# The last block of a chunked state scan reordered on TensorE and VectorE, with one block's statistics moved into the expert passes

## The reference

```
xn = LN(x)
u  = silu(causal_conv(xn @ Wx.T));  z = xn @ Wz.T              # 512 inner channels, 8 heads of 64
b, c = u @ Wb.T, u @ Wc.T;  dt = softplus(u @ Wdt.T + b_dt)
state_t = exp(dt_t * a) * state_(t-1) + dt_t * b_t (x) u_t     # a 64x64 state for each head
y_t = c_t . state_t + d * u_t
yn = (y - mean) / sqrt(var + eps)                              # over all tokens of a sequence, by head
s  = ((yn * gn_w + gn_b) * silu(z)) @ Wout.T
g  = silu(sum over 8 experts of gate * expert(their 1024 tokens of largest gate))
out = x + s * g
```

## Time and profile before

| | before |
|---|---|
| median of 3 runs | 1240.03 us (1238.38 to 1241.29) |
| the profiled execution | 1240.59 us |
| its span on the core | 1238.4 us |
| PE busy | 1211.5 us, 98% |
| DVE / POOL / ACT busy | 948.0 us, 77% / 792.0 us, 64% / 611.0 us, 49% |
| granted TensorE clock, mean | 0.994 |

### The profile page before, as it was taken

The page is one execution under the profiler, slowest core; times in us unless marked ns, Lnnn a source line. Parts: engine busy times, 40 slices in busy tenths (PEclk is TensorE's granted clock), DMA queues, the critical chain, the costliest instruction groups (busy, mean ns, idle before and its releaser), DMA issues.

```text
span 1238.4 us, 30811 instructions
## 1 busy us (share of the span) xinstructions
PE 1211.5 (98%) x12207; PEld 1015.2 (82%) x12207; DVE 948.0 (77%) x2030; ACT 611.0 (49%) x1277; POOL 792.0 (64%) x788
## 2 busy tenths in 40 slices
PE   8999999999999999999999997899999999999998
PEld 4666677888878888888888876789999889899998
DVE  7999876889876776777777775897778766776776
ACT  6999974434434353443443435334344332554453
POOL 4889845455555577767767755376666654576764
PEclk9999999999999999999999998999999999999999
DMA  9799758553544444454444365464444545799995
GB/s 296 261 339 354 291 201 183 179 168 130 162 156 158 152 153 148 147 180 154 163 162 155 130 196 157 144 148 89 107 95 90 104 86 119 236 321 329 339 321 173
DMA packets 124462, 231.33 MB, mean 187 GB/s; under 512 B 21280, under 2 KB 88096, under 8 KB 116128
## 3 DMA queue, kind: packets, MB, share of 16 engines
q1 hardware_dynamic: 111168, 212.08, 51.0%
q0 software_dynamic: 12288, 17.05, 8.0%
q10 hardware_dynamic: 864, 0.24, 0.1%
HBM read 147.81 MB, written 81.53 MB: 185 GB/s over the span
## 4 chain that ended last, share of the span: by engine, by line
PE 81%; DVE 9%; ACT 3%; issue 2%; DMA 2%; POOL 1%; SPq 1%; POOLq 0%; ACTq 0%; DVEq 0%
PE ps L1390 26%; PE ps L1736 9%; PE ps L1993 9%; PE ps L2227 7%; PE ps L2206 7%; PE ps L1471 4%; PE ps L1438 3%; PE ps L1498 3%; PE ps L1460 3%; PE ps L1482 2%; PE ps L1509 2%; PE ps L695 2%; DVE acc L324 1%; ACT tap L503 1%; DVE acc L335 1%
## 5 line engine op out<-in xcount | busy, mean ns | idle before, releaser
L1357 ACT ACTIVATE decay<-tap,ncum 128x128 f32<-128x128 f32 x344 | 105.5, 389 | 175.6 <-POOL tap L1268 175.6
L1921 POOL DMA_INDIRECT ffn_dram<-ob,idx x64 | 110.3, 1724 | 81.6 <-DVE ob L1840 67.3
L1151 DVE TENSOR_TENSOR x_dt<-ps,dt 128x512 f32<-128x512 f32 x64 | 44.3, 692 | 142.1 <-PE ps L1498 142.1
L1955 ACT ACTIVATE mid<-ps,b_up 128x512 f32<-128x512 f32 x96 | 66.0, 689 | 162.3 <-PE ps L1736 137.4
L1275 POOL TENSOR_TENSOR x_lo<-x,x_hi 128x512 fp32r<-128x512 f32 x56 | 75.4, 1346 | 98.7 <-ACT x_hi L1341 98.5
L1390 PE MATMUL ps<-x_hi,w_hi_c 128*128 128x512 f32 x240 | 99.4, 414 | 1.3 <-DVE state L1103 1.3
L1390 PE MATMUL ps<-x_hi,w_hi_b 128*128 128x512 f32 x240 | 99.9, 416 | 0.7 <-ACT bT L1346 0.7
L1297 POOL TENSOR_SCALAR yb<-x,dcol 128x512 f32<-128x512 f32 x64 | 44.8, 701 | 85.0 <-DMA y_dram<-yb 42.8
L2082 POOL TENSOR_SCALAR yc<-yc,gn_scale,gn_shift 128x512 f32<-128x512 f32 x56 | 76.9, 1385 | 32.0 <-DMA yc<-y_dram 32.0
L1390 PE MATMUL ps<-x_hi,w_lo_b 128*128 128x512 f32 x240 | 93.8, 391 | 1.9 <-issue 1.9
L1390 PE MATMUL ps<-x_lo,w_hi_b 128*128 128x512 f32 x240 | 95.0, 396 | 0.0
(11 more groups left out here) (319 smaller groups left out, 3961.0 us busy)
## 6 DMA issues: line engine op xcount, KB each, us to landing
tap<-cum_dram SPq DMA_DIRECT2D x43, 512.0 KB, 4.9
x_dram<-x SPq DMA_DIRECT2D x16, 1024.0 KB, 5.6
x<-x_dram SPq DMA_DIRECT2D x16, 1024.0 KB, 5.5
ecum_row<-ecum_dram SPq DMA_DIRECT2D x128, 128.0 KB
y_dram<-yb SPq DMA_DIRECT2D x16, 1024.0 KB, 4.6
yc<-y_dram SPq DMA_DIRECT2D x16, 1024.0 KB, 6.7
cum_row<-cum_dram SPq DMA_DIRECT2D x21, 512.0 KB
rows_dram<-xn SPq DMA_DIRECT2D x16, 512.0 KB, 3.3
```

Source lines behind the costliest of these rows:

```text
L1357: n = nc.scalar.activation(decay[g % 2][:, h, :], cum_row[g % NR][:, row, :], ACT.Exp, bias=t.ncum[:, g, h:h + 1])
L1921: pool.indirect_dma_start(out=t.ffn_dram, out_offset=bass.IndirectOffsetOnAxis(ap=t.idx[:, e, h * HC + c:h * HC + c + 1], axis=0), in_=ob[ ...
```

## The change

- PE, last block: `own_parts(g)` is moved ahead of `update(g)`; the wait for the state, which stood ahead of the second filler, is moved behind it, to just ahead of `state_parts(g)`. In chunks 20 to 59 the wait is moved from ahead of the c projection to ahead of `update(g)`.
- The state sum of chunk 61 goes to bank 5 in place of bank 7; so `update(61)` on PE waits for `mid` of slice 0 in place of `xg_lo`, while `update(62)` waits, as before, for two of them. Slices 3 and 4 wait for the states that slices 2 and 4 waited for.
- DVE, chunks 61 to 63: `x_dt`, `mix`, `b_w`, `update(g-1)`, the tail of the chunk, and `sums(g)` last. So the sums of y stand in the chunk's own turn, behind everything else of it.
- Block 14's four `bn_stats` leave chunks 60 to 63 and stand in the expert phase's pass 0, behind `split_down(0)`. SP's `load_down(1)` waits for them as well.
- ACT, chunk 0: `b_part(1, 0)` ahead of `decays(1)`.

```diff
     def added(g):
-        bank = ps_pc if g == LAST + 1 else ps_pb if g == LAST + 2 else ps_r
+        bank = ps_pb if g == LAST + 2 else ps_r
         return bank[:, LISTS:LISTS + MT * HD]
...
         def finish(g):
             dve.wait_ge(y_mm, g + 1)
             update(g)
             if LIST0 <= g < LIST1:
                 add_lists(g - LIST0, g)
+            sums(g)
+
+        def sums(g):
+            b, c = g // CH, g % CH
+            cols = slice(c * P, (c + 1) * P)
+            dve.wait_ge(y_mm, g + 1)
             if c == 0:
                 dve.wait_ge(dx_ready, b + 1)
...
-            if g % SPAN:
+            if g % SPAN and g <= LAST:
                 finish(g - 1)
             if not last:
                 dve.wait_ge(b_turned, updates(g) + 1)
...
+            if g > LAST:
+                update(g - 1)
...
-            if b:
+            if b and g < LAST:
                 if c == 0:
                     dve.wait_ge(y_ready, g)
                 v.bn_stats(t.ystat[:, b - 1, c, :], yb[(b - 1) % 2][:, c, :]).then_inc(stat_done, 1)
...
+            if g >= LAST:
+                sums(g)
         for g in range(NT):
             chunk(g)
-        finish(NT - 1)
...
         for g in range(NT):
             b, c = g // CH, g % CH
+            if g == 0:
+                b_part(b + 1, c)
             if g + 1 < NT:
                 decays(g + 1)
             if b + 2 < NB:
                 hi_part(b + 2, c)
             if b + 1 < NB:
-                b_part(b + 1, c)
+                if g:
+                    b_part(b + 1, c)
                 c_part(b + 1, c)
...
-            if g == LAST + 1:
-                pe.wait_ge(x.xg_lo_ready, 2 * s.KT)
-            elif g == LAST + 2:
-                pe.wait_ge(x.mid_ready, 2)
+            if g > LAST:
+                pe.wait_ge(x.mid_ready, g - LAST)
...
-            until(pe, state_ready, updates(g))
             if 1 <= g <= ROUNDS:
+                until(pe, state_ready, updates(g))
                 total(g - 1)
             elif SLOTS <= g < SLOTS + CH:
+                until(pe, state_ready, updates(g))
                 slots(c)
...
             until(pe, lists_read, listed(g))
+            until(pe, state_ready, updates(g) if g < LAST else updates(LAST))
             if LIST0 <= g < LIST1:
                 list_tiles(g - LIST0)
-            if not last:
+            if g < LAST and not last:
                 update(g)
...
             mm = own_parts(g)
+            if g >= LAST and not last:
+                update(g)
             if not first:
+                until(pe, state_ready, updates(g))
                 pe.wait_ge(c_dec_ready, g + 1)
                 mm = state_parts(g)
...
         elif e == 1:
             sp.wait_ge(t.y_ready, s.NT)
+            sp.wait_ge(t.stat_done, MT * (s.NB - 1))
...
-            if n in (0, 2, 4):
-                pe.wait_ge(t.state_ready, t.updates(s.NT - 3 + n // 2))
+            if n in (0, 3, 4):
+                pe.wait_ge(t.state_ready, t.updates(s.NT - 3 + n // 3 + n // 4))
...
-        def last_stats():
-            dve.wait_ge(t.y_ready, s.NT)
+        def last_stats(i):
+            b, y = t.y_ends[i]
+            dve.wait_ge(t.y_ready, s.NT // NB * (b + 1))
             for m in range(MT):
-                v.bn_stats(t.ystat[:, NB - 1, m, :], t.y_last[:, m, :]).then_inc(t.stat_done, 1)
+                v.bn_stats(t.ystat[:, b, m, :], y[:, m, :]).then_inc(t.stat_done, 1)
...
             if u == 0:
                 split_down(0)
+                last_stats(0)
                 dve.wait_ge(t.zero_stored, 16 * NB)
                 continue
...
             if u == STATS:
-                last_stats()
+                last_stats(1)
```

More of the change, by code:

```diff
@@ L1121, in finish @@
         def finish(g):
-            b, c = g // CH, g % CH
-            cols = slice(c * P, (c + 1) * P)
             dve.wait_ge(y_mm, g + 1)
@@ L1254, in _ @@
         sp.dma_start(t.y_dram[NB - 1], yb[(NB - 1) % 2][:, :, :]).then_inc(y_stored[(NB - 1) % 2], 16)
-    t.y_last = yb[(NB - 1) % 2]
+    t.y_ends = [(b, yb[b % 2]) for b in (NB - 2, NB - 1)]
     @block.gpsimd
```

## The result

| | before | after |
|---|---|---|
| median of 5 runs | 1240.03 us | 1248.10 us (1244.6 to 1250.37) |
| ratio | | 1.0078, 95% interval 1.0061 to 1.0094 |
| the profiled execution / its span | 1240.59 / 1238.4 us | 1250.37 / 1248.2 us |

A forecast was written before the change was run, and what follows sets the result against it. PE was taken to bound the kernel, DVE between 790 and 808.4 us. Terms: -0.65 - 0.95 - 0.30 + 2.40 + 2.35 = +2.85, so 1243.4 us against the profiled 1240.6, 1242.9 against the median; range 1237.5 to 1244.8.

The forecast's parts named there:

- ACT in chunk 0: Chunk 1: with b_part ahead of eight exponentials, PE's wait of 0.65 us for bT goes; gain 0.65 us.
- The state's wait in chunks 20 to 59: Chunk 58: the c projection starts at once, update(58) then waits only for b_w; gain 0.95 us.
- Chunk 60 and slice 0: Last block: own_parts(60) starts 0.65 us sooner, but the state is ready at the old time; gain at most 0.1 us.
- The new wait: Last block: update(61) waits for ACT to read slice 0 out; PE idle 4.3 us, clock falls, state_parts(61) 1.5 us late.
- The rest of the block: Last block from chunk 62 to DVE's last sums, replayed partly at half rate: gain 0.3 us, bounds +0.1 and -0.65.
- The statistics: Behind split_down(0): four bn_stats delay DVE's weighing by 2.40 us; PE's idle time ahead of 808.42 grows to about 3.1.
- The clock behind that: Behind 808 us: PE's clock falls after 3.1 us of idleness; cost 2.35 us, bounds 0 and 2.9.
- rival 1: Behind 808 us PE's clock holds despite 3.1 us of idleness: +0.5, so 1240.5 us; chance 0.27.
- load_down(1) at no cost: SP, expert phase: load_down(1) moves from 793 to about 802 us, behind the statistics; cost 0, at most 1 us.
- Rival 2: Clock back late both times, load_down(1) late, no gain in chunk 1: +5.45, so 1245.5 us; chance 0.08.
- Rival 3: Last block: cum_row(63) lands in 3.8 us, not 6.5; PE idles 1.6 us, not 4.3; -4.0 or -1.65 us; chance 0.15.
- Rival 4: Chunks 20 to 59: the removed state waits return as waits for b_w, worth 0.95 us at most; no chance stated.

The follow-up runs named there:

- kernel before with one more wait: The kernel before with a needless wait more on PE ahead of state_parts in every chunk, nothing moved: 1237.78 us, ratio 0.9989.
- second profile: The changed kernel profiled once more, with nothing altered: 1250.84 us in one profiled execution.
- early load: The changed kernel with SP loading cum_row(63) in chunk 60, ahead of its wait for the sums, the store and the other load: 1243.44 us, ratio 1.0034.
- old wait place: Changed kernel, PE's state wait of chunks 1 to 59 put back: 1243.05 us, ratio 1.0040; with bank 7 and statistics in chunk 61's gap too: 1236.39 us, 0.9984.
- second profile of the kernel before: The kernel before profiled once more, with nothing altered: 1237.59 us.

## Why the prediction was wrong

The direction was right in the forecast itself, though the chances put "the same" (0.46) ahead of "slower" (0.42), and three of its mechanisms are in the trace as described. The size was not: +8.1 us by the medians, +2.9 forecast. In the profiles it is +9.8 against +2.85; of the 7 us that were missed, 3.8 lie in the body of the scan and 3.2 in the last block.

- *ACT in chunk 0, gain 0.65.* The wait for `bT` is gone in every profile with this edit, and from chunk 1's transposes to chunk 2's PE takes 9.3 to 9.7 us in place of 10.2. Right. In the profile shown it was offset by the first row of cumulated decays, which came 0.6 us later.
- *The state's wait in chunks 20 to 59, gain 0.95.* This is the step that failed. I priced the wait's end in chunk 58 (0.86 us gained, and 0.55 left as a wait for `b_w`: right), and nothing for the stream of instructions that the edit changes in all chunks. The pauses rose from 2.3 to between 5.4 and 7.2 us. The body came out 2 to 5 us longer, not 0.95 shorter; putting the wait back removed it. So, with the gain of chunk 1 offset, the -1.60 of the first two terms became +2.2 in the profile.
- *Chunk 60 and slice 0, gain at most 0.1.* own_parts(60) starts 4.9 us behind chunk 60's transposes (4.8 forecast). But slice 0 starts 14.30 us behind them, 14.04 before: 0.3 late and not 0.1 early. It is 0.3 late as well where the clock held in both (11.8 us with update ahead of the sums, 11.5 in the kernel before with one more wait). The wait for `mid` hides that here.
- *The new wait.* Its mechanism, holder and idle time were right (4.3 forecast, 4.18 measured; 6.9 in the second profile), and undoing the bank brought the ratio from 1.0078 to 1.0016.
- *The rest of the block, -0.3.* Measured +2.9 (5.3 less the 2.4 of the statistics). This is the second step that failed: the holder was mis-sized. I took the one landing of rows 6, 6.7 us from issue to use, and the profiles of the changed kernel without the early load have 8.5 to 8.8, apart from the two with the old wait place (7.0 and 6.7). That is 1.8 of the 3.2 us. Another 0.4 is the half rate, which lasted 5.5 us, my dearer bound (the clock is 0.98 from 784 to 788). The other 1.0 are lags in my replay: the last sums start 17.7 us behind update(61), where it had 16.75. Against the second profile of the kernel before, the block is 8.2 us longer, and by the medians that profile counts as much as the first: I had taken the half-rate spell of the earlier trace rows at 775 for a part of the kernel, which it need not be.
- *The statistics, 2.40.* Measured 2.4 on DVE, with 3.15 us of idle time on PE (3.1 forecast). Right.
- *The clock behind that, 2.35 between 0 and 2.9.* Measured 2.3, and 1.1 to 1.5 in the five other profiles with that idle time in which it fell. It did not fall in two (429.93 and 430.01). So forecast and rival 1 are both seen, and the usual price is nearer to 1.3; that the 2.35 came out in the profile shown is luck.
- *load_down(1) at no cost.* Right: the fourth group waited for DVE's weighing alone.
- *Rival 2*, all prices at the upper end, gave 1245.5, and still fell short for want of the pauses and of the later landing. *Rival 3* would have needed a shorter landing. The early load shows that its mechanism is real, and it had the time right: `mid` ready 17.8 us behind chunk 60's transposes by rival 3, update(61) 18.0 behind them as measured. What it had wrong is PE's side: PE was idle for 3.8 us and not 1.6, as it came there sooner at full clock, and the clock did not stay up. *Rival 4* did not come about: the state wait did go.
- *Waits that the readings left out.* In the kernel before PE also waits 0.41 us for `b_w` ahead of update(62), and 0.18 us at 840.46 for DVE, where the prediction saw five waits in the last block and none behind 808.4. Neither changes the sum.
- *The Trainium skill's* estimate for a load (3.2 us by its page "DMA: Bandwidth & Descriptors", section "Anatomy of one DMA", as worked out in the prediction) was again far from the trace (8.5 us in the queue behind two others). That section gives its figures for single DMAs issued by GpSimd, and this load is SP's; the measurement decides.

What stays open: why the same load takes 6.7 us in some streams and 8.5 in others, and why an instruction packet comes too late in one stream and not in another. Of the load the traces tell two things. It took 8.6 us in the kernel before with one more wait too, at no cost there, so the new order of the last block is not needed for it. And from the store of y to the load's use the queues moved 2.92 MB in the kernel before and 3.39 in the changed one, at some 300 GB/s in both; the difference is about the store of zeros (512 KB) that SP issues behind the load.

## What to carry to other kernels

A wait that is moved in a loop can cost more than its own end, since it changes the stream of a densely issuing engine (one wait more cost nothing here, one moved cost 2 to 5 us): look for its waits without a releaser in the profile after, and compare them with those of a second profile of before. Before a sum is given another bank, follow what the bank's reader has in its own order ahead of the reading, back to its loads. Work taken out of one stretch should go into one where its engine has a gap; here a gap of 9 us, made by the reordering, was ahead of it, and the statistics went past it into the one stretch where VectorE was the bound.

## What the runs showed of the hardware

- PE's pauses without a releaser are a property of the kernel's stream: five of them (near 326, 346, 486, 607 and 694 us) come at the same places, to 3 us, in the profiles of the changed kernel and of its versions that differ from it in the last block alone, and come elsewhere once 64 waits are put ahead. They cost 2 to 8 us of 545.
- All 56 pauses of the scan's body in fourteen profiles end 2.2 to 3.0 us behind the start of a packet of the instruction queue, which has 63 of these in 554 us; most packets have no pause behind them.
- Behind the pause near 345 us the clock fell after 1.90 us of idleness (kernel before) and held after 2.81 (row of decays loaded earlier).
- Behind 3.1 us of idleness of a full-rate PE the clock fell in six of eight profiles, at a price of 1.1 to 2.3 us, and held in two; behind 0.7 us at the same place it did not fall in any of six. The same wait of 2.09 us in the same kernel was once followed by half rate and once not.
- A load of 512 KB, issued behind 1 MB and 768 KB, took between 6.6 and 8.8 us to its use; issued ahead of them it was out of the way.
